# Attention with top-32 and a quantised feed-forward: scales from the maxima alone, normalising by add and multiply, and the engines' orders written out anew

## What is computed

```python
def rmsnorm(x):
    return x * jax.lax.rsqrt(jnp.mean(x * x, axis=-1, keepdims=True) + EPS)

def act_quant(x):
    scale = 127.0 / jnp.clip(jnp.max(jnp.abs(x), axis=-1, keepdims=True), 1e-05)
    return jnp.clip(jnp.round(x * scale), -128.0, 127.0) / scale

def bitlinear(x, w, b):
    return jnp.einsum('bsd,fd->bsf', act_quant(rmsnorm(x)), weight_quant(w)) + b

# the two parts
q, k, v = layernorm(x) @ Wq.T + bq, ctx @ Wk.T + bk, ctx @ Wv.T + bv
vals, idx = jax.lax.top_k(q @ k.T / sqrt(256), 32)       # other scores: -inf
x = x + softmax(masked scores) @ v @ Wo.T + bo
x = x + bitlinear(gelu(bitlinear(layernorm(x), w1, b1)), w2, b2)
```

## Time and profile before

| | |
|---|---|
| time, median of 3 runs | 278.8 us (278.34 to 279.41) |
| the profiled execution, first to last instruction (span) | 277.2 us |
| TensorE busy | 262.5 us, 95% |
| VectorE busy | 230.2 us, 83% |
| ScalarE busy | 215.8 us, 78% |
| GpSimd busy | 165.0 us, 60% |
| mean granted clock of TensorE | 0.999 |

### The profile page before, as it was taken

The page is one execution under the profiler, slowest core; times in us unless marked ns, Lnnn a source line. Parts: engine busy times, 40 slices in busy tenths (PEclk is TensorE's granted clock), DMA queues, the critical chain, the costliest instruction groups (busy, mean ns, idle before and its releaser), DMA issues. The chain is left out here.

```text
span 277.2 us, 5366 instructions
## 1 busy us (share of the span) xinstructions
PE 262.5 (95%) x1527; PEld 230.4 (83%) x1527; DVE 230.2 (83%) x984; ACT 215.8 (78%) x323; POOL 165.0 (60%) x235
## 2 busy tenths in 40 slices
PE   7999999999999899999999999999999999799784
PEld 7999998998887788988898889888978898577463
DVE  2561868988979897989898989899989798989894
ACT  2567495586589988988799879987998899647762
POOL 3334409931888587849775887678767943612330
PEclk9999999999999999999999999999999999999999
DMA  6991010046000330025001500151004100610011
GB/s 223 316 342 40 4 38 0 1 79 151 2 2 0 77 78 0 0 69 125 0 4 45 139 5 4 38 140 18 0 1 124 31 1 2 151 38 5 0 38 38
DMA packets 29436, 16.42 MB, mean 59 GB/s; under 512 B 20445, under 2 KB 28190, under 8 KB 29406
## 3 DMA queue, kind: packets, MB, share of 16 engines
q1 hardware_dynamic: 28702, 15.02, 20.3%
q0 software_dynamic: 272, 0.79, 1.0%
q10 hardware_dynamic: 432, 0.26, 0.3%
HBM read 9.77 MB, written 2.10 MB: 43 GB/s over the span
## 5 line engine op out<-in xcount | busy, mean ns | idle before, releaser
L399 PE MATMUL bank<-vo,pT 128*128 128x257 f32 (+1 forms) x416 | 97.1, 381 | 2.4 <-ACT pT L1101 2.4
L399 PEld LDWEIGHTS bank<-vo,pT 128*128 128x128 f32 (+1 forms) x416 | 76.0, 190 | 15.1 <-ACT pT L1101 4.8
L1413 DVE MAX8 cand<-s_sb 128x8 f32<-128x50 f32 (+1 forms) x512 | 60.0, 201 | 1.6 <-issue 1.1
L258 PE MATMUL score<-k_high,q_low 128*128 128x400 f32 (+1 forms) x128 | 49.5, 387 | 0.0
L868 POOL TENSOR_TENSOR g<-g,b_bc 128x512 f32<-128x512 f32 x24 | 37.9, 1592 | 12.1 <-ACT g L1125 12.1
L258 PE MATMUL score<-k_low,q_high 128*128 128x400 f32 (+1 forms) x128 | 44.2, 346 | 0.0
L258 PE MATMUL score<-k_high,q_high 128*128 128x400 f32 (+1 forms) x128 | 44.0, 344 | 0.0
L1052 ACT ACTIVATE s_sb<-score 128x400 f32<-128x400 f32 x64 | 30.6, 504 | 10.2 <-PE score L258 10.1
L1101 ACT ACTIVATE pT<-bank 128x512 f32<-128x512 f32 x64 | 31.9, 514 | 4.2 <-PE bank L266 4.2
L1448 DVE SCALAR_TENSOR_TENSOR e_all<-s_sb,best,e_all 128x1601 f32<-128x1601 f32 x16 | 34.2, 2138 | 0.9 <-ACT e_all L1093 0.5
L266 PE MATMUL bank<-ident,e_all 128*128 128x128 f32 (+1 forms) x208 | 30.7, 273 | 2.6 <-ACT pT L1101 2.6
(11 more groups left out here) (162 smaller groups left out, 503.2 us busy)
## 6 DMA issues: line engine op xcount, KB each, us to landing
x_in<-in_x SPq DMA_DIRECT2D x16, 128.0 KB, 2.2
w_sb<-in_L_ffn_w SPq DMA_DIRECT2D x2, 1024.0 KB, 12.1
x_res<-in_x SPq DMA_DIRECT2D x16, 128.0 KB, 2.9
out<-o_sb SPq DMA_DIRECT2D x16, 128.0 KB, 2.0
ctx_sb<-in_ctx SPq DMA_DIRECT2D x2, 512.0 KB, 7.6
ctx_sb<-in_ctx SPq DMA_DIRECT2D x2, 256.0 KB, 4.1
b_bc<-in_L_ffn_b POOLq DMA_DIRECT2D x1, 512.0 KB, 7.6
w_q<-in_L_xattn_Wq SPq DMA_DIRECT2D x1, 256.0 KB, 2.8
```

The lines of the kernel that those rows point to most:

```text
L258: ins = pe.matmul(out, a, b, start=(i == 0), stop=(i == len(steps) - 1))
L399: ins = pe.matmul(bank[:, 0:DV], pT[0:n, t % 2, b * P:(b + 1) * P], vo[0:n, b, :], start=(b == 0), stop=(b == SB - 1))
L1413: ins = dve.max(cand[:, t % 2, k:CAND:PIECES], s_sb[:, t % 2, k * PIECE:end])
```

## The change

Scales. With x the centred row, max|x| * r and r are both multiples of r, so r drops out of the quantising factor: it is 127 / max(max|x|, a clip), two operations. scales_1 and scales_2 compute it, quantise_1 and quantise_2 wait for these two alone, and r and the undoing factor follow in dequant_1 and dequant_2, four operations, placed elsewhere in GpSimd's order. The clip becomes a constant. For tiles 14 and 15 tile_scales, tile_spread and tile_dequant do the same on VectorE.

Normalising. normalise_scale also makes minus the mean, one more operation on 128x2 elements; normalise adds it and multiplies. Operations with one step get a second, neutral one.

Orders. The rounds are gone: every engine's steps are listed one by one, in another order. hidden waits in addition for squares(t - 2).

The diff, cut; the listed orders stand here for the end of TensorE's and ScalarE's and the beginning of SyncE's.

```diff
@@ -46,7 +46,8 @@
 NCTX = -(-SB // 2)
 TOPK_STEPS = 2 * ROUNDS - 1
 DEPTH = (2, 4, 6, 8)
-ROW1, ROW2, X2S = 7, 7, 5
+ROW1, ROW2, X2S = 6, 6, 5
+CLIP1, CLIP2 = 1e-5 * EPS, 1e-5 * EPS ** 0.5
 LAST_ROUND = PAIRS + 2
 LAST = TILES - 2
 CTX_PARTS = ((0, 2), (2, 4), (4, 8), (8, 12))
...
-        ln1_r = sb("ln1_r", [P, 2, 2])
+        ln1_r = sb("ln1_r", [P, 3, 2])
         xn = sb("xn", [P, 2, D])
         q_full = sb("q_full", [P, DC, 2 * P])
         q_high = sb("q_high", [P, DC, 2 * P], F32R)
@@ -469,132 +470,286 @@
             turn_context(2)
...
             turn_weights(13, 3)
-            weighted(13, 1)
             weighted(13, 2)
             weighted(13, 3)
             scores(15, 3)
-            down(9)
             turn_weights(14, 0)
             turn_weights(14, 1)
             turn_weights(14, 2)
-            down(10)
             weighted(14, 0)
-            down(11)
+            turn_weights(14, 3)
+            weighted(14, 1)
             turn_y1(6)
-            weighted(14, 1)
+            weighted(14, 2)
+            weighted(14, 3)
             up(12, 0)
-            turn_weights(14, 3)
             up(12, 1)
             up(13, 0)
-            weighted(14, 2)
-            weighted(14, 3)
+            down(10)
+            up(13, 1)
+            down(11)
             turn_weights(15, 0)
             turn_weights(15, 1)
-            up(13, 1)
             turn_weights(15, 2)
             weighted(15, 0)
             weighted(15, 1)
             turn_weights(15, 3)
             weighted(15, 2)
             weighted(15, 3)
+            turn_y2(12, 0)
             turn_y1_tile(14)
+            turn_y2(12, 1)
+            turn_y2(13, 0)
+            turn_y2(13, 1)
+            down(12)
             up(14, 0)
             up(14, 1)
-            turn_y2(12, 0)
-            turn_y2(12, 1)
-            turn_y2(13, 0)
+            down(13)
             turn_y1_tile(15)
-            turn_y2(13, 1)
-            down(12)
             up(15, 0)
             up(15, 1)
-            down(13)
             hold_clock(23)
             turn_y2(14, 0)
             turn_y2(14, 1)
@@ -660,68 +815,68 @@
...
+            load_residual(0)
             load_x(1)
+            load_residual(1)
+            load_x(2)
+            load_x(3)
             turn_counts(0)
-            load_x(2)
+            turn_ffn_weights(0)
+            load_x(4)
             turn_counts(1)
-            turn_ffn_weights(0)
+            turn_ffn_weights(1)
             turn_counts(2)
-            load_x(3)
...
             def normalise_scale(j):
 
                 pool.wait_ge(ln1_step, (j + 1) * 4)
-                pool.tensor_scalar(ln1_r[:, 0, :], ln1_mv[:, :, 1], EPS, None, ALU.add).then_inc(ln1_row, 1)
-                pool.wait_ge(ln1_row, j * 2 + 1)
+                pool.tensor_scalar(ln1_r[:, 0, :], ln1_mv[:, :, 1], 1.0, EPS, ALU.mult, ALU.add).then_inc(ln1_row, 1)
+                pool.tensor_scalar(ln1_r[:, 2, :], ln1_mv[:, :, 0], -1.0, 0.0, ALU.mult, ALU.add).then_inc(ln1_row, 1)
+                pool.wait_ge(ln1_row, j * 3 + 2)
                 pool.tensor_tensor(ln1_r[:, 1, :], ln1_r[:, 0, :], minus_half[:, :], ALU.pow).then_inc(ln1_row, 1)
 
             def normalise(j, u):
 
-                pool.wait_ge(ln1_row, j * 2 + 2)
+                pool.wait_ge(ln1_row, j * 3 + 3)
                 if j:
                     wait_full(pool, ("q", j - 1))
-                pool.tensor_scalar(xn[:, u, :], x_in[:, u, :], ln1_mv[:, u, 0:1], ln1_r[:, 1, u:u + 1],
-                                   ALU.subtract, ALU.mult).then_inc(xn_ready, 1)
+                pool.tensor_scalar(xn[:, u, :], x_in[:, u, :], ln1_r[:, 2, u:u + 1], ln1_r[:, 1, u:u + 1],
+                                   ALU.add, ALU.mult).then_inc(xn_ready, 1)
 
             def split_queries(j):
...
+            def scales_1(j):
 
...
+                pool.tensor_scalar(row1[:, v, 0, :], cen_max[:, pair], CLIP1, 1.0 / 127.0, ALU.max,
+                                   ALU.mult).then_inc(row1_step, 1)
+                pool.wait_ge(row1_step, base + 1)
+                pool.tensor_tensor(row1[:, v, 1, :], row1[:, v, 0, :], minus_one[:, :], ALU.pow).then_inc(row1_step, 1)
+
+            def dequant_1(j):
+
+                v, base = j % 2, j * ROW1
+                pair = slice(2 * v, 2 * v + 2)
+                pool.tensor_scalar(row1[:, v, 2, :], ln2_mv[:, pair, 1], 1.0 + EPS, EPS * EPS, ALU.mult,
+                                   ALU.add).then_inc(row1_step, 1)
+                pool.wait_ge(row1_step, base + 3)
+                pool.tensor_tensor(row1[:, v, 3, :], row1[:, v, 2, :], minus_half[:, :], ALU.pow).then_inc(row1_step, 1)
+                pool.wait_ge(row1_step, base + 4)
+                pool.tensor_tensor(row1[:, v, 4, :], row1[:, v, 3, :], row1[:, v, 0, :], ALU.mult).then_inc(row1_step, 1)
+                pool.wait_ge(row1_step, base + 5)
+                pool.tensor_scalar(row1[:, v, 5, :], row1[:, v, 4, :], wmean[:, 0:1], 1.0, ALU.mult,
+                                   ALU.mult).then_inc(row1_step, 1)
 
             def quantise_1(j, u):
 
                 t = 2 * j + u
+                pool.wait_ge(row1_step, j * ROW1 + 2)
                 if j:
                     wait_full(pool, ("y1", j - 1))
-                pool.tensor_scalar(y1[:, u, :], cen[:, t % 4, :], row1[:, j % 2, 5, u:u + 1], MAGIC,
+                pool.tensor_scalar(y1[:, u, :], cen[:, t % 4, :], row1[:, j % 2, 1, u:u + 1], MAGIC,
                                    ALU.mult, ALU.add).then_inc(y1_ready, 1)
...
+            def scales_2(j):
 
...
+                pool.tensor_scalar(row2[:, v, 0, :], g_max[:, 0:2], CLIP2, 1.0 / 127.0, ALU.max,
+                                   ALU.mult).then_inc(row2_step, 1)
+                pool.wait_ge(row2_step, base + 1)
+                pool.tensor_tensor(row2[:, v, 1, :], row2[:, v, 0, :], minus_one[:, :], ALU.pow).then_inc(row2_step, 1)
+
+            def dequant_2(j):
+
+                v, base = j % 2, j * ROW2
+                pool.wait_ge(g_sq_ready, (j + 1) * 2)
+                pool.tensor_scalar(row2[:, v, 2, :], g_ssq[:, 0:2], 1.0 / F, EPS, ALU.mult, ALU.add).then_inc(row2_step, 1)
+                pool.wait_ge(row2_step, base + 3)
+                pool.tensor_tensor(row2[:, v, 3, :], row2[:, v, 2, :], minus_half[:, :], ALU.pow).then_inc(row2_step, 1)
+                pool.wait_ge(row2_step, base + 4)
+                pool.tensor_tensor(row2[:, v, 4, :], row2[:, v, 3, :], row2[:, v, 0, :], ALU.mult).then_inc(row2_step, 1)
+                pool.wait_ge(row2_step, base + 5)
+                pool.tensor_scalar(row2[:, v, 5, :], row2[:, v, 4, :], wmean[:, 1:2], 1.0, ALU.mult,
+                                   ALU.mult).then_inc(row2_step, 1)
+
...
                 act.wait_ge(row1_step, (j + 1) * ROW1)
...
                     act.wait_ge(y2_ready, t - 1)
+                    act.wait_ge(g_sq_ready, t - 1)
                 src = wait_full(act, ("up", t, h))
-                drain(act.activation(g[:, u, h * BANK:(h + 1) * BANK], src[:, :], ACT.Copy, scale=row1[:, j % 2, 6, u:u + 1]),
+                drain(act.activation(g[:, u, h * BANK:(h + 1) * BANK], src[:, :], ACT.Copy, scale=row1[:, j % 2, 5, u:u + 1]),
                       ("up", t, h))
 
...
@@ -1155,19 +1356,19 @@
             def quantise_2(t):
 
                 j = t // 2
-                act.wait_ge(row2_step, j * ROW2 + 6)
+                act.wait_ge(row2_step, j * ROW2 + 2)
                 if t >= 2:
                     act.wait_ge(y2_lowered, t - 1)
-                act.activation(y2_raised[:, t % 2, :], g[:, t % 2, :], ACT.Identity, scale=row2[:, j % 2, 5, t % 2:t % 2 + 1],
+                act.activation(y2_raised[:, t % 2, :], g[:, t % 2, :], ACT.Identity, scale=row2[:, j % 2, 1, t % 2:t % 2 + 1],
                                bias=magic_col[:, 0:1]).then_inc(y2_ready, 1)
 
...
+            gelu(11)
             exp_all(14)
             take_weights(13, 2)
-            copy_scores(15, 0)
+            take_weights(13, 3)
+            quantise_2(10)
             copy_scores(15, 1)
-            take_weights(13, 3)
             copy_scores(15, 2)
-            quantise_2(10)
             lower_2(10)
+            quantise_2(11)
+            take_weights(14, 0)
+            lower_2(11)
             copy_scores(15, 3)
-            quantise_2(11)
-            lower_2(11)
-            take_weights(14, 0)
             take_weights(14, 1)
+            take_weights(14, 2)
+            squares(10)
             exp_all(15)
-            take_weights(14, 2)
+            take_weights(14, 3)
             take_y1(6)
-            take_weights(14, 3)
+            squares(11)
             gelu(12)
             take_weights(15, 0)
             take_weights(15, 1)
+            gelu(13)
             squares(12)
-            gelu(13)
             take_weights(15, 2)
             squares(13)
             take_weights(15, 3)
-            take_y1_tile(14)
             quantise_2(12)
             quantise_2(13)
```

(16 more changed lines are left out.)

1265 lines of the change are left out of this document (859 added, 406 removed).

## The result

The kernel after takes 277.11 us (median) against 278.72 for the kernel before in the same comparison: ratio 0.995, interval 0.9928 to 0.9972. An execution can fall into a slower state, so the ratios are formed over the fast runs alone and need not be the quotient of two medians. So the change is worth 1.4 to 2.2 us; 6.9 us was forecast. The tail gave what was forecast; the middle gave nothing.

What follows compares the result with a forecast made beforehand. The number of matmuls on TensorE was taken to set the pace, leaving only stops and tail to give: 5.0 + 1.9 = 6.9 us off 278.8, so 271.9 us, range 267.5 to 278.5.

Steps and rivals of the forecast that it cites:

- The tail: Work after the last attention tile: 2.3 us gained by a shorter VectorE chain, 0.4 charged against it, net 1.9 us.
- Scales and normalisation: GpSimd's shorter scale chain and add-multiply sweep (0.5 us taken, from 1230 ns): 0 us each in the sum.
- Rival three: The normalise edit does nothing, the sweep stays at 1.23 us: 272.7 us, chance 0.10.
- The lock: VectorE's weigh and GpSimd's sweeps exclude each other; VectorE's 4.0 us of waits counted as margin, not gain.
- Rival two: Slower: eight meetings on the shared ports fall on VectorE, making release late by 4.3 us: 281.2 us, chance 0.14.
- The orders of the middle: Rewritten engine orders, 42.90 to 257.05 us: of 7.8 us of stops 2.7 remain, gain 5.1, say 5.0 us.
- The steps and their number stay: Premise for all five engines' orders: they are written out anew, while the steps and their number are unchanged.
- 0.4 us a pair in three pairs, 1.2 us: Stops left in the middle other than those at tiles 14 and 15: 1.2 us in all.
- Tile 14: 0.7, tile 15: 0.8: TensorE's stops for take_weights: tile 14's shrinks from 1.72 + 0.16 to 0.7 us, and 0.8 us is left at tile 15.
- Rival one: The middle gives nothing, stops move elsewhere because ScalarE serves the same work in a fixed order: 276.9 us, chance 0.20.
- load_x(4) ahead of turn_counts(1): Added wait on SyncE for normalise(3, 1) before the step release(1) needs: 0 to 3.1 us once, taken as 0.
- TensorE's busy share outside the tail: Sign that the forecast holds: above 96% in the profile after.

Runs made afterwards that it cites:

- e6: Kernel with before's orders up to the last attention tile and after's arithmetic and tail, but normalise again by subtract and multiply: 276.17 us, 0.9865 of before.
- e7: Kernel with before's orders up to the last attention tile and after's arithmetic and tail, but dequant_1 ahead of both quantisations in seven pairs: 276.29 us, 0.988 of before.
- e3: Kernel before, with release(t) moved directly behind largest_count(t) in the loop and in tiles 13 and 14: 282.96 us, 1.0129 of before.
- e12: Kernel after with eight releases covered, dequant_1 of pairs 1, 2, 4 behind quantisations, early GELU table, best_8(5,0) behind release(4), split_queries(6) earlier: 271.63 us, 0.9723 of before.
- e8: Before's orders up to the last attention tile, after's arithmetic and tail, plus early GELU table and take_weights(14,0), (14,1) ahead of lower_2(11): 274.93 us, 0.9838 of before.

## Why the prediction was right, and where it was wrong

*The tail: right.* 1.9 us forecast, 20.15 - 18.16 = 2.0 us measured (1.5 in the longest of the three profiles). The step named for it too: ScalarE's last two GELU halves, VectorE's scales, and the last quantise_half:

```profile
265.18 1.27 ACT L1342 ACTIVATE s_sb<-s_sb 128x512 f32<-128x512 f32 x2
...
267.83 0.81 ACT L1371 ACTIVATE y_raised<-s_sb,magic_col,row 128x512 f32<-128x512 f32 x1 [0.21 <-DVE row L1899]
```

From 265.18 + 1.27 = 266.45 to 267.83 there are 1.38 us; 1.4 was forecast, 3.70 it had been.

*Scales and normalisation: right.* Nothing measurable in the loop by themselves (e6, e7). Add-multiply takes 549 ns in the mean, where 0.5 us was taken. Rival three is out. The edit also moved the first scalar from ln1_mv to ln1_r; that it is the subtraction which costs is likely but not shown apart from this. The Trainium skill, GPSIMD Engine Reference, section 3.1, has a body of up to two operations bound by the port at 1.03 cycles an element and names no dearer pair; add-multiply at 549 and multiply-add at 506 ns (quantise_1 in the same trace) fit that, the sweep with subtract and multiply at 1230 does not, and there the measurement decides.

*The lock: right in kind, short in scope.* weigh's mean fell from 2138 to 1977 ns, 2.6 us in sixteen sweeps where 4.0 were at stake, and short of the 1.95 us named as a sign; add_bias from 1592 to 1316. Rival two, VectorE paying more, did not come. What the step left out is that the change makes GpSimd's chains smaller and later, and that a step of 0.26 us pays as much (1.7 us more) as a sweep of 1.23 (2.87, 1.6 more). I allowed only for long partners. The Trainium skill, SBUF — State Buffer, section "SBUF: two separate sides", has the lock held for a whole instruction by whichever starts first; 132.16 against 132.24 agrees, and the page makes no exception for a small partner.

*The orders of the middle: wrong.* This is the step that failed, "Orders", with its sum 7.8 - 2.7 = 5.1. In the prediction's own measure 5.51 us idle and some 1.4 us hidden in nine stops remain between head and tail, 6.9 where it had 2.7, and the head took 1.2 more. Three of its terms, and one it lacked:

- *The steps and their number stay.* They do, but what stands beside what does not. A step's cost was taken to go with the step. In the loop of before VectorE idles 0 us at a release that has candidates beside it, 0.6 to 1.0 us where only the end of centre covers it; bare it idles about 1.0 us and nothing runs meanwhile (e3). The trace of before held no bare release in the loop, but its rows had the 0.9 us from largest_count's end to the signal in them, hidden. 14.3 - 7.5 = 6.8 us more of VectorE's time stood idle that way in after; in e3 9.6 us more made the kernel 3.6 us longer. The other steps whose neighbours changed are the ends of dequant_1 under weigh, 1.93 and 1.79 us in place of 0.26, and the copies at tile 15, below.
- *0.4 us a pair in three pairs, 1.2 us.* It was 3.66 us between head and tile 14, idle time alone. There was no row for the 1.2; it was a hope that new waits would be smaller than the old ones. The lower bound that the prediction itself gave, zero, was the place to stand.
- *Tile 14: 0.7, tile 15: 0.8.* Tile 14 came out at 0.55 us, so the order did mend what it was seen to mend. Tile 15 took 1.6 us, 1.46 of it idle. There I saw that gelu(12) stands ahead of the copies, as it did before, table load included, when the stop was 0.48 us idle. What I left out is that up(13, 1) no longer stands between the transposes.
- *The head.* I counted from 42.90 us on and took the head as given. The wait for release(0), late and uncovered, made 0.89 of the 1.2 us of new idle time there.

Rival one had the time, 276.9, and the words "the stops move to other places", but not the reason: it named ScalarE's fixed order, and the new stops are for VectorE's and GpSimd's steps as well. load_x(4) ahead of turn_counts(1) cost nothing, as taken: release(1) signals at 55.65 us and TensorE, which had stood for q_full until then, takes it at 57.54.

One of the signs I named was no sign. TensorE's busy share outside the tail is 248.15 of 256.44 us, 96.8%; before it was 97.0% already. Of the others, xn's sweep and the last quantise_half came as named; one stop for take_weights over 1 us stayed (1.46), and a release of VectorE came second in TensorE's waits, which was the sign of being wrong.

The reserve was there: e12, with the orders of after but for thirteen moved steps and a one-column GELU, ends the last attention tile at 252.19 us where "near 252" was forecast, from the keys 4.7 us sooner than before. That the size agrees so closely is in part luck, since the 1.2 us had no row. What was wrong is that this diff collects it.

## What to carry to other kernels

A rewritten order is not a list of old costs in new places: look in the trace for what is free only because of its neighbour (a register fetch and branch beside a queued step, a table load while TensorE has another product to do) and price it bare where the new order separates the two. When two engines exclude each other, move the long sweep away from whatever the critical engine will ask for next, not from the longest partner; a step of two columns pays the whole sweep. And take stops out several at a time, tracing after each: alone the edits gave 1.3 and 2.3 us, together 5.9, since VectorE's by themselves shifted a sweep onto GpSimd's quantisations.

## What the runs showed of the hardware

- A value fetched into a register and a branch on it cost VectorE 0.9 us from the end of the reduction to the signal (TENSOR_LOAD itself 309 ns in the median, up to 1276 ns at tile 0); with nothing to run meanwhile VectorE idles 0.97 to 1.0 us in most tiles of e3, with candidates between 0, and with centre between 0.6 to 1.0 (before).
- A GpSimd step on 128x2 that begins 0.08 us behind VectorE's 1601-element sweep lasts 1.93 us in place of 0.26; the sweep loses nothing (1.88 us).
- On GpSimd, 128x256: subtract and multiply 1230 ns in the median (before), add and multiply 549 ns in the mean (after), with the first scalar in another tensor.
- In e8 and e12 a one-column GELU fetches the table (1.28 us) while ScalarE would wait for hidden(12), and gelu(12) runs without a load.
- The first product for the keys begins up to 1.1 us apart in executions of the same kernel (10.36 to 11.44 us in after), so two profiles should be laid on each other there and not at their start.
